# A transformer block in one line of slots: a new order table, a shorter gelu block, and two transfers in place of eight for the reciprocals

## The reference

```python
shift_a, scale_a, gate_a, shift_m, scale_m, gate_m = jnp.split(jax.nn.silu(c) @ W_mod + b_mod, 6, axis=-1)
q, k, v = split(modulate(_ln(x), shift_a, scale_a) @ W_qkv + b_qkv)
x = x + gate_a[:, None] * (softmax(q k^T * scale) v @ W_proj + b_proj)
q_c = _ln(x) @ W_qc + b_qc;  k_c, v_c = split(_ln(context) @ W_kvc + b_kvc)
x = x + softmax(q_c k_c^T * scale) v_c @ W_cproj + b_cproj
h = gelu(modulate(_ln(x), shift_m, scale_m) @ W_mlp1 + b_mlp1) @ W_mlp2 + b_mlp2
return x + gate_m[:, None] * h
```

## Time and profile before

| | |
|---|---|
| median of 3 runs | 1634.08 us (1629.98 to 1639.45) |
| the profiled execution, its own time | 1633.06 us |
| its span, first to last instruction | 1631.3 us |
| busy: PE, DVE, ACT, POOL | 1406.4, 1145.2, 1130.6, 718.4 us |
| mean granted TensorE clock | 0.958 of full speed |

### The profile page before, as it was taken

How to read it: one execution, slowest core, us unless ns; L and a number is a source line. 1 busy time by engine, 2 the same in 40 slices (tenths; PEclk the granted TensorE clock), 3 DMA queues, 4 the chain that set the end, 5 groups by cost and what they waited for, 6 DMA issues and landing times.

```text
span 1631.3 us, 40543 instructions
## 1 busy us (share of the span) xinstructions
PE 1406.4 (86%) x15090; PEld 918.4 (56%) x15090; DVE 1145.2 (70%) x2477; ACT 1130.6 (69%) x2343; POOL 718.4 (44%) x1005
## 2 busy tenths in 40 slices
PE   3477899989999899999999999999999998988764
PEld 1234466666666666666665666666666566655433
DVE  4657877777887777777788777777778877765411
ACT  3144687877777777787777778777777777776541
POOL 2232345454455445445445544544544544543222
PEclk8678999999999999999999999999999999999877
DMA  5122333233233233233323333323232323321100
GB/s 157 51 74 74 94 92 90 91 89 95 81 97 92 86 89 96 87 90 90 93 86 96 89 90 90 95 90 88 90 99 81 95 85 90 86 74 59 44 28 20
DMA packets 166118, 138.08 MB, mean 85 GB/s; under 512 B 45921, under 2 KB 156674, under 8 KB 165922
## 3 DMA queue, kind: packets, MB, share of 16 engines
q1 hardware_dynamic: 165922, 135.48, 27.9%
HBM read 56.60 MB, written 9.57 MB: 41 GB/s over the span
## 4 chain that ended last, share of the span: by engine, by line
PE 33%; SPq 20%; ACT 20%; DMA 11%; DVE 8%; issue 5%; POOL 3%; POOLq 0%; ACTq 0%; DVEq 0%
SPq L436 12%; PE o_ps L678 8%; SPq L469 6%; ACT G L835 6%; PE dense_ps L351 5%; PE max_ps L643 4%; PE dense_ps L353 4%; PE dense_ps L352 4%; DMA r_dram_cross<-o_r_cross 4%; DMA o_rb_cross<-r_dram_cross 3%; ACT g_split L789 3%; DVE mx_self L1002 3%; PE exp_ps L660 3%; ACT probs L804 3%; PE dense_ps L585 3%
## 5 line engine op out<-in xcount | busy, mean ns | idle before, releaser
L804 ACT ACTIVATE probs<-exp_ps 128x512 f32<-128x512 f32 x1024 | 558.1, 602 | 247.8 <-PE exp_ps L660 244.6
L1002 DVE TENSOR_REDUCE mx_cross<-max_ps 128x2 f32<-128x512 f32 x512 | 328.4, 683 | 202.6 <-PE max_ps L643 198.4
L1002 DVE TENSOR_REDUCE mx_self<-max_ps 128x2 f32<-128x512 f32 x512 | 329.0, 684 | 62.6 <-PE max_ps L643 59.3
L1110 POOL TENSOR_TENSOR o_n_self<-o_n_self,o_rb_self 128x512 f32<-128x512 f32 x32 | 40.6, 1269 | 267.1 <-DMA o_rb_self<-r_dram_self 267.1
L1143 POOL TENSOR_TENSOR g_split<-G,g_split 128x512 f16<-128x512 f32 x128 | 144.7, 1156 | 28.2 <-ACT g_split L789 26.6
L660 PE MATMUL exp_ps<-q_stack_cross,k_stack_cross 50*128 50x256 f16 x1024 | 100.7, 274 | 63.8 <-ACT probs L804 55.4
L351 PE MATMUL dense_ps<-mlp_hi,g_split 128*128 128x256 f16 x512 | 141.9, 277 | 6.4 <-POOL g_split L1143 3.9
L678 PE MATMUL o_ps<-probs,V_cross 128*32 128x256 f32 x2048 | 141.9, 396 | 0.6 <-ACT o_sb_cross L812 0.6
L351 PE MATMUL dense_ps<-xt,mlp_hi 128*128 128x256 f16 x512 | 140.7, 275 | 1.9 <-DVE xt L964 1.9
L678 PE MATMUL o_ps<-probs,V_self 128*32 128x256 f32 x2048 | 142.2, 397 | 0.0
L352 PE MATMUL dense_ps<-mlp_lo,g_split 128*128 128x256 f16 x512 | 140.7, 275 | 0.0
(11 more groups left out here) (212 smaller groups left out, 3351.3 us busy)
## 6 DMA issues: line engine op xcount, KB each, us to landing
q_stack_self<-split_q SPq DMA_DIRECT2D x192, 64.0 KB, 2.6
k_stack_self<-split_k SPq DMA_DIRECT2D x192, 64.0 KB, 2.5
k_stack_cross<-split_kc SPq DMA_DIRECT2D x192, 64.0 KB, 2.6
q_stack_cross<-split_qc SPq DMA_DIRECT2D x192, 64.0 KB, 2.6
X<-in_x SPq DMA_DIRECT2D x32, 256.0 KB, 2.8
Ctx<-in_ctx SPq DMA_DIRECT2D x32, 256.0 KB, 3.0
rows_a<-rows_a_dram SPq DMA_DIRECT2D x32, 256.0 KB, 4.1
o_n_self<-o_sb_self SPq DMA_DIRECT2D x64, 128.0 KB, 3.0
```

The lines of the kernel that those rows point to most:

```text
L804: nc.scalar.activation(probs[:, (t + ab) % 8], exp_ps[:, ab], ACT.Exp).then_inc(exp_taken[kind], 1)
L1002: nc.vector.tensor_reduce(mx[kind][:, :, ab, t // 2], max_ps[:, ab].rearrange("p (q k) -> p q k", q=2), AX_X, ALU.max).then_inc(max_taken[ ...
```

## The change

There are four parts. First, iterations are gone: `Timeline` puts every step of every batch at a moment on one line of slots, and the tenant of a bank, the exp block and the max block before a given one are looked up in the order of that line. Second, `PLAN` and `BANK` have new numbers (so `q`, `k` and `v` of a batch stand ahead of that iteration's gelu or beside it, and not behind it), and the start of the max and exp blocks is in the table too. Third, `AHEAD` moves steps of batches 0, 1, 2 and 27 to 31 by so many slots (positive is earlier), each batch by numbers of its own. Fourth, in the gelu block a gelu of one column is done first, which loads the table; the four copies `gelu_hi` leave the block and are steps `g_hi_0` to `g_hi_3` with slots of their own; and `o_sb` and `r_dram` have their middle dimensions swapped, so that `r_fetch` needs two DMAs of 64 rows of 2 KB in place of eight of 16 rows, and the numerators' gather reads rows of 2 KB in place of two of 1 KB.

```diff
 PLAN = {
...
-    "k": (-1, 1, 6), "k_hi": (-1, 1, 6), "k_lo": (-1, 1, 8), "stack_k": (-1, 1, 10), "v": (0, 0, 7),
...
+    "mlp1_2": (4, 1, 0), "mlp1_3": (4, 1, 0), "gelu": (4, 1, 0), "g_hi_0": (4, 1, 5), "g_hi_1": (4, 1, 7),
...
+def moment(step, n):
+
+    lag, half, slot = PLAN[step]
+    return ((n + lag) * 2 + half) * TILES + slot - AHEAD.get(n, {}).get(step, 0)
...
+class Timeline:
...
+                for t in range(0, TILES, 2):
+                    self.max[moment(f"max_{kind}", n) + t] = (kind, b, t)
+                    self.exp[moment(f"exp_{kind}", n) + t] = (kind, b, t)
+                for g in range(4):
+                    self.av[moment(f"exp_{kind}", n) + AV_AFTER + 4 * g] = (kind, b, g)
+            for step in PLAN:
+                if step[:4] not in ("max_", "exp_"):
+                    self.steps[step, moment(step, n)] = b
...
-                flat = r_dram[kind][b.u].rearrange("j i g (a e) -> (j i g a) e", e=32)
+                flat = r_dram[kind][b.u].rearrange("j g (a e) -> (j g a) e", e=32)
...
                 for g in range(2):
-                    for j in range(4):
-                        src = r_dram[kind][b.u, j, :, g]
-                        (i_step, i_n), (e_step, e_n) = [tuple(v) for v in src.ap]
-                        nc.sync.dma_start(o_rb[kind][64 * g + HD * j:64 * g + HD * j + HD],
-                                          bass.AP(tensor=src.tensor, offset=src.offset,
-                                                  ap=[[0, HD], [i_step, i_n], [e_step, e_n]])).then_inc(o_rb_in[kind][b.u], 16)
+                    rows = r_dram[kind][b.u, :, g]
+                    (j_step, j_n), (e_step, e_n) = [tuple(v) for v in rows.ap]
+                    nc.sync.dma_start(o_rb[kind][64 * g:64 * g + 64],
+                                      bass.AP(tensor=rows.tensor, offset=rows.offset,
+                                              ap=[[j_step, j_n], [0, HD], [e_step, e_n]])).then_inc(o_rb_in[kind][b.u], 16)
...
+                if (b := due("gelu")):
+                    nc.scalar.activation(gelu_primer[:], neg_half[:, 0:1], ACT.Gelu_apprx_tanh)
+                    wait_count(act, g_lo, b.n * 4)
+                    for i in range(4):
+                        act.wait_ge(ready[f"mlp1_{i}"], b.n + 1)
...
+                        last.then_inc(taken[f"mlp1_{i}"], 1)
+                for i in range(4):
+                    if (b := due(f"g_hi_{i}")):
+                        gelu_hi(b, i)
```

More of the change, by code:

```diff
@@ L59 @@
-    "mlp1_2": 2, "mlp1_3": 1, "vc": 1, "t1": 0, "proj": 0, "mlp2": 1, "q": 0, "k": 2, "v": 1, "t2": 2,
-}
-DENSE = {n: BANK[n] for n in sorted(BANK, key=lambda n: PLAN["mlp2_0" if n == "mlp2" else n][1:])}
-MAX_LAG = {"self": 0, "cross": 2}
-EXP_LAG = {"self": 0, "cross": 3}
-EXP_START = 6
+    "m_self": 0, "m_cross": 2, "qc": 2, "cproj": 0, "tc": 1, "kc": 0, "t3": 0, "mlp1_0": 0, "mlp1_1": 2,
+    "mlp1_2": 1, "mlp1_3": 2, "vc": 2, "t1": 0, "proj": 2, "mlp2": 1, "q": 2, "k": 1, "v": 1, "t2": 2,
+}
@@ L91, in lag_of, with __init__ @@
-def lag_of(unit):
-    return PLAN["mlp2_0" if unit == "mlp2" else unit][0]
-def previous(it, order, lags, name):
-    order = list(order)
-    at, where = order.index(name), it
-    for _ in range(7 * len(order)):
-        at -= 1
-        if at < 0:
-            at, where = len(order) - 1, where.before()
-        b = where.batch(lags[order[at]])
-        if b is not None:
-            return order[at], b
-    return None
+    def __init__(self, n):
+        self.n, self.pair, self.u = n, n // 2, n % 2
@@ new lines, in moment, with __init__, predecessors @@
+def moment(step, n):
+    lag, half, slot = PLAN[step]
+    return ((n + lag) * 2 + half) * TILES + slot - AHEAD.get(n, {}).get(step, 0)
+class Timeline:
+    def __init__(self, batches, kinds):
+        self.steps, self.max, self.exp, self.av = {}, {}, {}, {}
+        for n in range(batches):
+            b = Batch(n)
+            for kind in kinds:
+                for t in range(0, TILES, 2):
[6 more added lines that the diff above has]
+                    self.steps[step, moment(step, n)] = b
+        assert len(self.steps) == batches * (len(PLAN) - 2 * len(kinds))
+        assert len(self.max) == len(self.exp) == batches * len(kinds) * TILES // 2
+        def predecessors(turns):
+            turns = [t[1:] for t in sorted(turns)]
+            return dict(zip(turns[1:], turns))
+        every = [(kind, n) for kind in kinds for n in range(batches)]
+        self.max_before = predecessors((moment(f"max_{k}", n), k, n) for k, n in every)
+        self.exp_before = predecessors((moment(f"exp_{k}", n), k, n) for k, n in every)
+        self.tenant_before = {}
+        for bank in set(BANK.values()):
+            self.tenant_before.update({unit[1:]: before[1:] for unit, before in predecessors(
+                (moment("mlp2_0" if u == "mlp2" else u, n), i, u, n)
+                for i, u in enumerate(PE_ORDER) if BANK[u] == bank for n in range(batches)).items()})
+        self.first = min(at for _, at in self.steps)
+        self.last = max(max(at for _, at in self.steps), max(self.av))
```

720 lines of the change are left out of this document (362 added, 358 removed), and 35 rows, old and new, of tables (AHEAD, PLAN).

## The result

The changed kernel takes 1557.05 us, median of 4 runs (1554.96 to 1558.06); the kernel before took 1632.03 us beside it (4 runs, 1627.48 to 1639.45). The ratio is 0.953, with a 95% interval from 0.950 to 0.956. The profiled execution took 1557.84 us, its span is 1555.7 us.

What follows compares the result with a forecast made beforehand. The gelu block delays SyncE's queue, that the o chain, and that TensorE. From 1633.1 us, 44 (middle), 10 (fill) and 13 (drain) were taken off: 1566 us, range 1530 to 1606 (the forecast case's own 1545 to 1588).

Steps and rivals of the forecast that it cites:

- The fetch: Two fetches for eight in the o chain: from start to product 4.2 us for 5.17, gain 1.0 us (0.1 to 2.7).
- 2.6 us to spare: Cross product 4.0 us earlier against a 0.62 us wait ahead of `cproj`; 2.6 us left over after the period's shortening.
- The rival "slower": Reciprocal rows share too few DMA engines, so the fetch lands late; 1780 us with one engine; chance 0.06.
- The gelu block: ScalarE's exponentials behind the gelus end 1.8 us earlier against a 1.42 us wait; TensorE's 37.0 us of waits go.
- Its cover: One-column gelu and table load lie inside ScalarE's 1.16 us wait and the 1.3 us after; uncovered at most 12 us.
- q ahead of the gelu: SyncE no longer waits for a split behind the gelus; the gather of denominators starts up to 2.98 us earlier.
- The new order: In the middle, 26.3 us of waits on maxima stay and new waits for VectorE cost 13 us, between nothing and 26.3.
- the middle's sum: Gain in the middle: 37.0 + 16.1 - 13 + 4 = 44 us, a period of 43.7 us.
- Fill and drain: Stretches before the first output and after the last full batch: 10 us shorter (rounds 5 to 13) and 13 us (5 to 30).
- the rounds alone: In the drain, four rounds with gelus and o chain in series save 1.8 + 1.0 us each, 11 us.
- the 2 us of batch 31: In the drain, batch 31 gains about 2 us of 14.7 us between value copies, through exponentials ahead of the gelu.
- One sign of being wrong: Named beforehand as showing the forecast wrong: a wait for the product of the o chain larger than before.

## Why the prediction was right, and where its steps were not

The forecast was 1566 us, and 1557 us came, 9 us under it. The mechanism named as the bound was the right one: the gelu block delays SyncE's queue, the queue the o chain, and the chain TensorE. Point by point:

*The fetch: the step that failed.* The prediction took 4.2 us from start to product for 5.17, a gain of 1.0 us, and set beside it a rule by which the fetch runs on four engines and gains 0.1 us. The packet counts and a busy share of 0.25 show four engines. In the old queue the two forms are alike (5.50 and 5.59 us, a gain of 0.1 us, as that sum said), and in the new queue the cross fetch takes 0.8 us more than before (6.40 us). The term had the wrong sign. The 0.4 us that the sum adds behind the packets have no row either; with one fetch on eight engines the busy share is near nothing from about 3.0 us after the start, and the self product starts at 3.97 us, so nearer 1 us. The "2.6 us to spare" were reckoned on the wrong path. They hold for TensorE, whose wait for `ot_cross` is 0.2 us, but the copy of the same product stands in ScalarE's queue ahead of exponentials. ScalarE waits for the product 56.1 us, 21.7 before, and 20.3 us of waits for `probs` stay. The rival "slower" had the right mechanism, too few engines, but not its size, and put a loss only beyond 10 us from start to product. One fetch on eight engines wins 30 us more.

*The gelu block.* Predicted were the 37.0 us of waits for `probs`, gone; 16.7 us of them went. In the new order the block is worth 27.6 us over the whole run, measured by putting it back, 20.5 of them through the primer. The prediction priced table and copies as one, 1.8 us a batch, and told of the primer only its cost (at most 12 us); it is the larger part of the gain. Its cover was right: 0.20 us, within the wait for `mlp1`.

*q ahead of the gelu.* The wait for `split_q` went, and `ot_cross` with it: 15.9 us of the 16.1 predicted. What the order gave is larger than that term, since q back behind the block, in an order made for it ahead, costs 134.6 us. Parts of the change can't be priced one by one and added: the copies outside cost some 70 us in the old order and bring 10 at most in the new.

*The new order: a term of the wrong sign.* 13 us of new waits were predicted, half of the 26.3 us that maxima cost. No new kind came; the waits for maxima fell to 17.0 us, and small waits from 7.1 to 2.7. So the middle's sum (44 us, and 45.7 measured) came out by luck, through two errors that cancel: 20.3 us of `probs` that stayed, and 22.3 us of maxima that were priced at 13 more and became 9.3 fewer.

*Fill and drain.* 10 us were predicted and 11.4 measured in the fill; 5.1 of them are not there with an empty `AHEAD`. 13 us were predicted and 18.4 measured in the drain, within the 5 to 30 given; 11.1 are not there with an empty table. In that one profile the drain gains 7.3 us (201.5 less 194.2), less than the 11 us predicted for the rounds alone, and the table gives more than the 2 us of batch 31, if the middle does not pay for it.

*What was to be seen.* Outputs 43.7 us apart, the first near 238 us, the wait for `ot_cross` under 5 us and two issues for eight: all so. The wait for `probs` under 5 us was not so, and the drain is 183.1 us for 188. One sign of being wrong did show: a wait for the product of the o chain larger than before, ScalarE's 56.1 us for 21.7.

## What to carry to other kernels

Before several small transfers are merged into one, count the engines that each form uses (the completions in the queue's packet count tell it, or the busy share of the engines while it moves alone), and look at what large transfers are issued just behind it. Two merged transfers on four engines were no better than eight on sixteen; one whose source began with a dimension of eight was. A step moved in one engine's queue must be followed to the engines that wait for its result: the same copies, moved out of the same block, cost some 70 us in one order, through what stood behind them in GpSimd's queue, and nothing in another. An activation of one column with the next table's function is a cheap way to load that table inside a wait; alone, in the old order, it was worth 1.4%.

## What the runs showed that was not expected

A fetch that copies the same row to many partitions follows the same count of engines as any other: its repeated dimension of 16 doesn't help when it is not the first. Two such fetches together kept only four engines busy (a share of 0.25 with both under way). In a quiet queue two fetches on four engines took as long as eight on sixteen (5.50 and 5.59 us, issue time included), because six issues fewer make up for it; with large transfers close behind they took 0.8 us more than without, and the median landing of an unrelated store there went from 2.3 to 5.5 us. And idle time of TensorE can cost twice: in the two runs in which it is idle longest in the middle (150 us with q ahead in the old order, 148 us with q behind in the new), its granted clock there is 0.96 and 0.98 for 1.00, and as many matmuls take 44 and 29 us longer.
